# Exp of the scores from PSUM, Sign as conversion, scaled features signalled per chunk

## The chip, the cores and the metric

One of the NeuronCores of a Trainium2 chip runs the kernel. The metric is the time of an execution on the device in microseconds (us), as the median of several runs. Engines: PE multiplies matrices and writes PSUM; DVE (VectorE), ACT (ScalarE) and POOL (GpSimd) work elementwise; SP (SyncE) only issues transfers. ACT, SP and POOL each have a queue on which they issue DMA transfers. Engines wait for each other through semaphores. SBUF and PSUM have 128 partitions; PSUM has 8 banks of 512 fp32 per partition.

## What is computed

A graph attention layer with residual and layer norm: N = 4096 nodes, D = 128 features, a dense adjacency matrix of int32 (64 MB) with 0 and 1.

```
s_i = x @ attn[:128]; s_j = x @ attn[128:]
e = leaky_relu(s_i + s_j.T, negative_slope=0.2)
e = e + where(adj > 0, 0, -1e9)
y = x + softmax(e, axis=1) @ x
out = (y - mean(y)) / sqrt(var(y) + 1e-5)      # per row
```

## The kernel before

The softmax is taken apart. With m the largest s_j, exp(leaky(s_i + s_j)) is, up to a factor of the row i that falls out in the division, exp(0.2 (s_j - m)) times max(q_i, r_j), where r_j = exp(0.8 (s_j - m)) and q_i = exp(-0.8 relu(s_i + m)). So DVE makes, for a **chunk** c of 128 nodes j and a **block** n of 512 nodes i, the weights max(q_row, r_j) * mask in one scalar_tensor_tensor (`weigh`, L658), 128x512, and PE multiplies them by xj = d_j * x (with d_j itself as a 129th column for the denominator). Four matmuls (`product`, L784), one for each 128 of the 512 rows, sum into four PSUM banks; the trace shows each as two records. There are 8 blocks of 32 chunks, 256 chunks. `q_row` holds q for all i in 8 pieces of 512; block n uses piece n.

The adjacency comes in 32 **pieces** g of 2 MB, four to a block, each worth 8 chunks. A piece is four transfers of 512 KB: SP issues two (LOW_HALF), ACT two (HIGH_HALF), in `load_piece` (L251 in the trace), and piece g is issued only when piece g-2 has landed and its buffer is free. Pieces from 2 on are converted from int32 to uint8 by ACT (`to_bytes`, L388 and L393, as Sigmoid(200 x - 100)), pieces 0 and 1 by DVE (L567, L554). DVE turns the bytes (stream transpose, `turn` L549, `turn_half` L562) and then weighs. On DVE the order is written out: after the sixth chunk of piece g (TURN_AT = 5) comes the turn of piece g+1. For the pieces in HALVED conversion and turn go in two halves of four chunks, the second half being turned after chunk SECOND_HALF_AT. After chunk 13 of a block comes the residual of the block before (L591 to L609). Weights may run 12 chunks ahead of PE (W_SLOTS).

Before the loop: PE turns x (L758) and computes the scores s_i, the same on all partitions, in eight pieces of 512 into PSUM banks (`s_i_piece`, L769); DVE and ACT compute s_j, its maximum m (`smax`), below_max = s_j - m. ACT makes d_j, r_j, and then for each s_i piece Relu(score + m) into q_row (L365), and Exp(-0.8 q) in place, for piece 0 at once (`q_factors`, L371) and for the other seven in one instruction later. It scales x into xj in four stripes of 8 chunks (`scale_xj`, L377) and signals each stripe. PE begins the loop when stripe 0 is scaled, weights 0 are ready and four s_i pieces have left PSUM, since the loop's first four banks (0 to 3) hold scores until then.

ACT runs all this in program order, its transfers included: a `load_piece` is issued where it stands in ACT's program. After the loop over a block ACT and POOL normalise its rows and POOL stores them.

## Time and profile before

| | us |
|---|---|
| median of 3 runs | 267.55 |
| lowest, highest | 266.38, 269.02 |
| the profiled execution | 266.52 |
| its span, first to last instruction | 264.7 |

| engine | busy us | share |
|---|---|---|
| PE | 248.3 | 94% |
| DVE | 237.0 | 90% |
| ACT | 172.6 | 65% |
| POOL | 36.0 | 14% |

| costliest lines | what | count | busy us | mean ns |
|---|---|---|---|---|
| L784 PE | product | 2048 | 231.6 | 276 (overlapping) |
| L658 DVE | weigh | 256 | 171.4 | 741 |
| L393 ACT | conversion of a piece | 28 | 103.9 | 3709 |
| L549 DVE | turn of a piece | 29 | 36.0 | 1241 |

The transfers move 71.67 MB, 271 GB/s over the span. Times of single instructions are from the profiled execution and count from its span's start. Matmul records overlap, so their spacing and not their duration gives PE's rate; a few can be missing. "Idle before" is the time an engine stood before an instruction, with what ended it. PEclk is the granted clock of PE as a share of 2.4 GHz.

### The profile page before, as it was taken

How to read it: one execution, taken by the hardware profiler on the slowest of the kernel's cores; microseconds unless marked ns; L12 is line 12 of the kernel's file. 1: busy time of each engine (PE TensorE's matmuls, PEld its weight loads, DVE VectorE, ACT ScalarE, POOL GpSimd, SP SyncE). 2: the span in 40 equal slices, each digit the busy share in tenths (PEclk: the TensorE clock that was granted, in tenths of full speed). 3: DMA queues.
4: the chain of work that ended last, by engine and by line, in shares of the span. 5: the costliest groups of instructions: out<-in, count | busy, mean ns of one | idle time of the engine just before them, and what ended most of it. 6: DMA issues, size and time to landing. Idle time of an engine off the chain costs nothing.

```text
span 264.7 us, 5321 instructions
## 1 busy us (share of the span) xinstructions
PE 248.3 (94%) x2117; PEld 242.1 (91%) x2117; DVE 237.0 (90%) x382; ACT 172.6 (65%) x249; POOL 36.0 (14%) x75
## 2 busy tenths in 40 slices
PE   5894999999999999999999999999999999999980
PEld 5643999999999989999999999999999999999980
DVE  1889988699989899999999999999999999999652
ACT  1479998655496549755985579755975497566410
POOL 1000000000033001400042003300330023003413
PEclk9799899999999999999999999999999999999996
DMA  7999999999999999999999999999999999930101
GB/s 188 316 346 299 297 224 283 308 299 297 298 270 287 332 303 288 305 352 311 303 308 349 307 311 297 316 330 295 307 294 344 297 313 310 349 110 2 41 0 42
DMA packets 70172, 71.67 MB, mean 271 GB/s; under 512 B 2817, under 2 KB 68610, under 8 KB 70146
## 3 DMA queue, kind: packets, MB, share of 16 engines
q1 hardware_dynamic: 34562, 34.67, 47.5%
q10 hardware_dynamic: 34560, 34.67, 47.1%
q0 software_dynamic: 1024, 1.97, 2.4%
q8 instruction: 17, 0.28, 0.5%
q14 instruction: 9, 0.07, 0.1%
HBM read 69.21 MB, written 2.10 MB: 269 GB/s over the span
## 4 chain that ended last, share of the span: by engine, by line
PE 63%; DMA 23%; ACT 6%; ACTq 2%; DVE 2%; issue 1%; POOL 1%; SPq 0%; DVEq 0%
PE psum L784 60%; DMA adj_in<-in_adj_dram 21%; DMA x_raw<-in_x_dram 2%; PE psum L758 2%; ACT xj L377 2%; ACT q_row L365 2%; ACTq L251 2%; ACT mask_bytes L393 1%; PE psum L769 1%; POOL out_dram L259 1%; DVE mask_t L549 0%; ACT L388 0%; DVE x_raw L603 0%; ACT x_raw L451 0%; DVE weights L658 0%
## 5 line engine op out<-in xcount | busy, mean ns | idle before, releaser
L784 PEld LDWEIGHTS psum<-xj,weights 128*128 128x128 f32 x2048 | 230.8, 193 | 6.8 <-ACT xj L377 4.6
L784 PE MATMUL psum<-xj,weights 128*128 128x129 f32 x2048 | 231.6, 276 | 5.4 <-ACT xj L377 3.8
L658 DVE SCALAR_TENSOR_TENSOR weights<-q_row,r_j,mask_t 128x512 f32<-128x512 f32 x256 | 171.4, 741 | 0.1
L393 ACT ACTIVATE mask_bytes<-adj_in,sig_bias 128x4096 uint8<-128x4096 int32 x28 | 103.9, 3709 | 61.1 <-DMA adj_in<-in_adj_dram 60.9
L549 DVE STREAM_TRANSPOSE mask_t<-mask_bytes 128x1024 uint32<-128x1024 uint32 x29 | 36.0, 1241 | 6.9 <-ACT mask_bytes L393 6.5
L312 POOL TENSOR_SCALAR neg_mean<-total 128x4 f32<-128x4 f32 x7 | 1.6, 222 | 181.5 <-ACT x_raw L401 181.5
L321 POOL DMA_DIRECT2D out_dram<-x_raw x28 | 14.6, 526 | 21.5 <-ACT x_raw L415 21.4
L415 ACT ACTIVATE x_raw<-x_raw,offset,rstd 128x128 f32<-128x128 f32 x28 | 11.4, 479 | 2.8 <-POOL offset L318 2.8
L408 ACT ACTIVATE unused<-x_raw,neg_mean 128x128 f32<-128x128 f32 x28 | 10.9, 390 | 2.5 <-POOL neg_mean L312 2.5
L316 POOL TENSOR_TENSOR rstd<-variance,half 128x4 f32<-128x4 f32 x7 | 9.9, 1411 | 0.6
L377 ACT ACTIVATE xj<-x_raw,d_j 128x128 f32<-128x128 f32 x32 | 9.7, 390 | 0.0
L603 DVE SCALAR_TENSOR_TENSOR x_raw<-psum,rden,x_raw 128x128 f32<-128x128 f32 x32 | 9.2, 345 | 0.4
L758 PEld LDWEIGHTS psum<-ident,x_raw 128*128 128x128 f32 x32 | 5.1, 181 | 4.4 <-DMA x_raw<-in_x_dram 2.8
L388 ACT ACTIVATE mask_bytes<-adj_in,sig_bias 128x2048 uint8<-128x2048 int32 x4 | 7.8, 1995 | 1.0 <-DMA adj_in<-in_adj_dram 1.0
L401 ACT ACTIVATE x_raw<-x_raw 128x128 f32<-128x128 f32 x28 | 8.2, 293 | 0.0
L758 PE MATMUL psum<-ident,x_raw 128*128 128x128 f32 x32 | 6.0, 345 | 2.2 <-DMA x_raw<-in_x_dram 2.2
L769 PE MATMUL psum<-adj_in,attn_iw 128*128 128x512 f32 x16 | 7.7, 593 | 0.0
L348 ACT COPY adj_in<-psum 128x512 f32<-128x512 f32 x8 | 4.3, 579 | 3.7 <-PE psum L758 3.7
L512 DVE TENSOR_TENSOR adj_in<-x_raw,attn_j 128x1024 f32<-128x1024 f32 x4 | 4.7, 1218 | 2.0 <-DMA x_raw<-in_x_dram 2.0
L591 DVE TENSOR_SCALAR rden<-psum 128x4 f32<-128x4 f32 (+2 forms) x10 | 1.6, 156 | 5.2 <-PE psum L784 5.2
L459 ACT ACTIVATE deviations<-moments,eps 128x1 f32<-128x1 f32 x2 | 0.6, 294 | 8.5 <-DVE moments L627 8.5
L562 DVE STREAM_TRANSPOSE mask_t<-mask_bytes 128x512 uint32<-128x512 uint32 x6 | 4.3, 709 | 1.9 <-ACT mask_bytes L388 1.9
(61 smaller groups left out, 66.5 us busy)
## 6 DMA issues: line engine op xcount, KB each, us to landing
adj_in<-in_adj_dram ACTq DMA_DIRECT2D x64, 512.0 KB, 11.4
adj_in<-in_adj_dram SPq DMA_DIRECT2D x64, 512.0 KB, 10.0
out_dram<-x_raw POOLq DMA_DIRECT2D x28, 64.0 KB, 5.4
x_raw<-in_x_dram ACTq DMA_DIRECT2D x4, 256.0 KB, 5.9
x_raw<-in_x_dram SPq DMA_DIRECT2D x4, 256.0 KB, 6.8
out_dram<-x_raw POOLq DMA_DIRECT2D x4, 32.0 KB, 1.8
out_dram<-x_raw SPq DMA_DIRECT2D x4, 16.0 KB, 1.8
out_dram<-x_raw ACTq DMA_DIRECT2D x4, 16.0 KB, 2.1
```

The lines of the kernel that those rows point to most:

```text
L316: nc.gpsimd.tensor_tensor(rstd[:, 0:K], variance[:, 0:K], half[:, 0:K], ALU.pow).then_inc(rstd_ready, 1)
L321: pool.dma_start(out_v[g, q, :, :], x_raw[B * q:B * (q + 1), g * K:(g + 1) * K, :].rearrange("b k d -> b (k d)")).then_inc(stored, 16)
L377: last = nc.scalar.activation(xj[:, c, 0:D], x_raw[:, c, :], ACT.Copy, scale=d_j[:, c:c + 1])
L393: nc.scalar.activation(mask_bytes[:, g % BYTE_SLOTS, :, :, :], adj_in[:, g % ADJ_SLOTS, :, :, :], ACT.Sigmoid, bias=sig_bias[:], scale=200 ...
L408: last = nc.scalar.activation(unused[:, k, :], tile(g * K + k), ACT.Square, bias=neg_mean[:, k:k + 1], accum_out=square_sum[:, k:k + 1])
L415: last = nc.scalar.activation(tile(g * K + k), tile(g * K + k), ACT.Identity, bias=offset[:, k:k + 1], scale=rstd[:, k:k + 1])
L549: nc.vector.transpose(dst.rearrange("p f (r a) -> p r f a", a=B), src).then_inc(mask_ready, 1)
L603: nc.vector.scalar_tensor_tensor(tile(n * K + t), banks[(n * K + t) % 8][:, 0:D], rden[:, t:t + 1], tile(n * K + t), ALU.mult, ALU.add).th ...
L658: nc.vector.scalar_tensor_tensor(weights[:, slot_of(n, c), :], q_row[:, n * BANK:(n + 1) * BANK], r_j[:, c:c + 1], mask_t[:, (n * PIECES + ...
L758: last = nc.tensor.transpose(banks[XT_BANK + m % 4][:, k * P:(k + 1) * P], x_raw[:, m * K + k, :], ident[:])
L769: nc.tensor.matmul(banks[bank][:, :], attn_iw[:], xT[:, rb * BANK:(rb + 1) * BANK], start=True, stop=True).then_inc(s_i_in_psum, 1)
L784: return nc.tensor.matmul(banks[(n * K + t) % 8][:, 0:D1], weights[:, slot_of(n, c), t * P:(t + 1) * P], xj[:, c, 0:D1], start=(c == 0), s ...
```

## The change

- **q directly from PSUM.** smax gets a third column, -0.8 m, made by one more DVE operation. ACT computes Exp(-0.8 score - 0.8 m) from PSUM in one instruction per piece (`q_piece`); Relu and the Exp over SBUF are gone. Without the Relu q can be above 1, where it should be 1.
- **min in place of mult.** The weights are min(max(q, r), mask). The mask is 0 or 1 and r at most 1, so this is 0 where there is no edge and cuts q at 1 where there is one.
- **Sign in place of Sigmoid** in the conversion of the adjacency, without bias and scale; the memset of the bias goes.
- **xj per chunk.** ACT signals every scaled chunk, and PE waits in block 0 for the chunk that it needs. Chunk 0 is scaled right behind q piece 0, chunks 1 to 7 behind the fourth q piece, 8 to 11 before the first conversion; the other twenty follow in fours around the half conversions of pieces 2 and 3. The last four q pieces are made behind pieces 2 and 4.
- **The first matmuls in reverse order.** Chunk 0's four matmuls go to banks 3, 2, 1, 0, each waiting for one more q piece.
- **ACT's transfers.** The two quadrants of piece 2 are issued apart, behind q piece 0 and behind the second; piece 3 is issued behind chunk 7; for halved pieces, piece g+2 is issued between the halves.
- **Piece 4 is halved too,** and the second half is turned after the fourth chunk instead of the third. DVE waits for the q piece of its own block alone, PE for all eight at block 1.

```diff
@@ -45,8 +45,8 @@
     MASK_SLOTS = 6
     W_SLOTS = 12
     BY_DVE = 2
-    SECOND_HALF_AT = 2
-    HALVED = (0, 2, 3)
+    SECOND_HALF_AT = 3
+    HALVED = (0, 2, 3, 4)
     TURN_AT = 5
     RESIDUAL_AT = 13
     LAST = 8
@@ -104,7 +104,7 @@
         below_max = sb("below_max", [P, CHUNKS], fp32)
         r_j = sb("r_j", [P, CHUNKS], fp32)
         d_j = sb("d_j", [P, CHUNKS], fp32)
-        smax = sb("smax", [P, 2], fp32)
+        smax = sb("smax", [P, 3], fp32)
         rden = sb("rden", [P, T], fp32)
         total = sb("total", [P, T], fp32)
         neg_mean = sb("neg_mean", [P, T], fp32)
@@ -116,7 +116,6 @@
         moments = sb("moments", [P, T, 2], fp32)
         deviations = sb("deviations", [P, T], fp32)
         offset = sb("offset", [P, T], fp32)
-        sig_bias = sb("sig_bias", [P, 1], fp32)
         eps = sb("eps", [P, 1], fp32)
 
 
@@ -169,8 +168,8 @@
         max_spread = sem("max_spread")
         max_found = sem("max_found")
         below_max_ready = sem("below_max_ready")
+        max_scaled = sem("max_scaled")
         factors_ready = sem("factors_ready")
-        s_i_ready = sem("s_i_ready")
         q_ready = sem("q_ready")
         xj_scaled = sem("xj_scaled")
         bytes_ready = sem("bytes_ready")
@@ -301,7 +300,6 @@
             nc.gpsimd.affine_select(out=ident[:], in_=ident[:], compare_op=ALU.not_equal, fill=1.0, base=0,
                                     pattern=[[-1, P]], channel_multiplier=1).then_inc(consts_ready, 1)
             nc.gpsimd.memset(half[:], -0.5)
-            nc.gpsimd.memset(sig_bias[:], -100.0)
             nc.gpsimd.memset(eps[:], EPS)
             nc.gpsimd.memset(rden[:], 0.0)
             nc.gpsimd.memset(worst[:], 0.0).then_inc(worst_ready, 1)
@@ -359,41 +357,34 @@
             nc.scalar.activation(r_j[:], below_max[:], ACT.Exp, scale=1 - SLOPE)
             nc.scalar.activation(xj[:, :, D], below_max[:], ACT.Exp, scale=SLOPE)
 
-            def s_i_piece(rb):
+            def q_piece(rb):
 
                 act.wait_ge(s_i_in_psum, S_I_BY_PE.index(rb) + 1)
-                nc.scalar.activation(q_row[:, rb * BANK:(rb + 1) * BANK], banks[S_I_BANK[rb]][:, :],
-                                     ACT.Relu, bias=smax[:, 1:2]).then_inc(s_i_ready, 1)
-
-            def q_factors(first, stop):
-
-                act.wait_ge(s_i_ready, stop)
-                nc.scalar.activation(q_row[:, first * BANK:stop * BANK], q_row[:, first * BANK:stop * BANK], ACT.Exp,
-                                     scale=SLOPE - 1).then_inc(q_ready, stop - first)
-
-            def scale_xj(st):
-
-                for c in range(st * SC, (st + 1) * SC):
-                    last = nc.scalar.activation(xj[:, c, 0:D], x_raw[:, c, :], ACT.Copy, scale=d_j[:, c:c + 1])
-                last.then_inc(xj_scaled, 1)
-
-            def to_bytes(g):
+                nc.scalar.activation(q_row[:, rb * BANK:(rb + 1) * BANK], banks[S_I_BANK[rb]][:, :], ACT.Exp,
+                                     bias=smax[:, 2:3], scale=SLOPE - 1).then_inc(q_ready, 1)
+
+            def scale_xj(first, stop):
+
+                for c in range(first, stop):
+                    nc.scalar.activation(xj[:, c, 0:D], x_raw[:, c, :], ACT.Copy, scale=d_j[:, c:c + 1]).then_inc(xj_scaled, 1)
+
+            def bytes_may_go(g):
 
                 act.wait_ge(adj_loaded[g % ADJ_SLOTS], 16 * Q * (g // ADJ_SLOTS + 1))
                 if g >= BYTE_SLOTS:
                     act.wait_ge(mask_ready, g - BYTE_SLOTS + 1)
-                if g in HALVED:
-                    for f in range(PF):
-                        part = slice(f * P, (f + 1) * P)
-                        half_bytes = nc.scalar.activation(mask_bytes[:, g % BYTE_SLOTS, :, :, part],
-                                                          adj_in[:, g % ADJ_SLOTS, :, :, part],
-                                                          ACT.Sigmoid, bias=sig_bias[:], scale=200.0)
-                        half_bytes.then_inc(act_half_ready if f == 0 else bytes_ready, 1)
-                else:
-                    nc.scalar.activation(mask_bytes[:, g % BYTE_SLOTS, :, :, :], adj_in[:, g % ADJ_SLOTS, :, :, :],
-                                         ACT.Sigmoid, bias=sig_bias[:], scale=200.0).then_inc(bytes_ready, 1)
-                if g + IN_FLIGHT < ALL_PIECES:
-                    load_piece(act, HIGH_HALF, g + IN_FLIGHT)
+
+            def half_to_bytes(g, f):
+
+                part = slice(f * P, (f + 1) * P)
+                half_bytes = nc.scalar.activation(mask_bytes[:, g % BYTE_SLOTS, :, :, part],
+                                                  adj_in[:, g % ADJ_SLOTS, :, :, part], ACT.Sign)
+                half_bytes.then_inc(act_half_ready if f == 0 else bytes_ready, 1)
+
+            def to_bytes(g):
+
+                nc.scalar.activation(mask_bytes[:, g % BYTE_SLOTS, :, :, :], adj_in[:, g % ADJ_SLOTS, :, :, :],
+                                     ACT.Sign).then_inc(bytes_ready, 1)
 
             def sum_rows(g):
                 act.wait_ge(y_ready, g * K + K)
@@ -417,21 +408,40 @@
                 last.then_inc(out_ready, 1)
 
             act.wait_ge(worst_ready, 1)
-            s_i_piece(0)
-            q_factors(0, 1)
-            load_piece(act, HIGH_HALF, 2)
-            for rb in S_I_ORDER[1:4]:
-                s_i_piece(rb)
-            scale_xj(0)
-            for rb in S_I_ORDER[4:]:
-                s_i_piece(rb)
-            q_factors(1, RB)
+            act.wait_ge(max_scaled, 1)
+            q_piece(0)
+            load_piece(act, HIGH_HALF[0:1], 2)
+            act.wait_ge(factors_ready, 1)
+            scale_xj(0, 1)
+            q_piece(S_I_ORDER[1])
+            load_piece(act, HIGH_HALF[1:2], 2)
+            q_piece(S_I_ORDER[2])
+            q_piece(S_I_ORDER[3])
+            scale_xj(1, PC)
             load_piece(act, HIGH_HALF, 3)
-            scale_xj(1)
+            scale_xj(PC, PC + K)
             for g in range(BY_DVE, ALL_PIECES):
-                to_bytes(g)
-                if g < BY_DVE + 2:
-                    scale_xj(g)
+                bytes_may_go(g)
+                if g in HALVED:
+                    half_to_bytes(g, 0)
+                    load_piece(act, HIGH_HALF, g + IN_FLIGHT)
+                    if g < PIECES:
+                        scale_xj(g * PC - K, g * PC)
+                    half_to_bytes(g, 1)
+                    if g < PIECES:
+                        scale_xj(g * PC, g * PC + K)
+                else:
+                    to_bytes(g)
+                    if g + IN_FLIGHT < ALL_PIECES:
+                        load_piece(act, HIGH_HALF, g + IN_FLIGHT)
+                if g == PIECES - 2:
+                    q_piece(S_I_ORDER[4])
+                    q_piece(S_I_ORDER[5])
+                elif g == PIECES - 1:
+                    scale_xj(CHUNKS - K, CHUNKS)
+                elif g == PIECES:
+                    q_piece(S_I_ORDER[6])
+                    q_piece(S_I_ORDER[7])
                 if g % PIECES == PIECES - 1 and g > PIECES:
                     sum_rows(g // PIECES - 1)
                     sum_squares(g // PIECES - 1)
@@ -535,6 +545,7 @@
             nc.vector.reduce_max(smax[:, 1:2], banks[MAX_BANK][:, 0:P], X).then_inc(max_found, 1)
             dve.wait_ge(max_found, 1)
             nc.vector.tensor_scalar(below_max[:], s_j[:], smax[:, 1:2], None, ALU.subtract).then_inc(below_max_ready, 1)
+            nc.vector.tensor_scalar(smax[:, 2:3], smax[:, 1:2], SLOPE - 1, None, ALU.mult).then_inc(max_scaled, 1)
 
             def turn(g):
 
@@ -658,10 +669,10 @@
                 nc.vector.scalar_tensor_tensor(
                     weights[:, slot_of(n, c), :], q_row[:, n * BANK:(n + 1) * BANK], r_j[:, c:c + 1],
                     mask_t[:, (n * PIECES + c // PC) % MASK_SLOTS, c // K % PF, :, c % K],
-                    ALU.max, ALU.mult).then_inc(weights_ready, 1)
+                    ALU.max, ALU.min).then_inc(weights_ready, 1)
 
             for n in range(BLOCKS):
-                dve.wait_ge(q_ready, 1 if n == 0 else RB)
+                dve.wait_ge(q_ready, S_I_ORDER.index(n) + 1)
                 for c in range(CHUNKS):
                     g = n * PIECES + c // PC
                     if c % PC == 0 and g in HALVED:
@@ -788,17 +799,17 @@
             for n in range(BLOCKS):
                 last_chunks = LAST if n == BLOCKS - 1 else 0
                 for c in range(CHUNKS - last_chunks):
-                    if n == 0 and c % PC == 0:
-                        pe.wait_ge(xj_scaled, c // PC + 1)
+                    if n == 0:
+                        pe.wait_ge(xj_scaled, c + 1)
                     pe.wait_ge(weights_ready, n * CHUNKS + c + 1)
                     if c == 0:
-                        if n == 0:
-                            pe.wait_ge(s_i_ready, 4)
-                        elif n == 1:
-                            pe.wait_ge(s_i_ready, RB)
-                        else:
+                        if n == 1:
+                            pe.wait_ge(q_ready, RB)
+                        elif n > 1:
                             pe.wait_ge(y_ready, (n - 1) * K)
-                    for t in range(K):
+                    for t in reversed(range(K)) if n == 0 and c == 0 else range(K):
+                        if n == 0 and c == 0:
+                            pe.wait_ge(q_ready, K - t)
                         last = product(n, c, t)
                     last.then_inc(weights_used, 1)
             for t in range(K):
```

ACT from the first q piece on, before (x3 stands for three alike; the waits are in brackets):

```order
L365 ACTIVATE q_row<-psum,smax 128x512 [waits s_i_in_psum,worst_ready]
L371 ACTIVATE q_row<-q_row 128x512 [waits s_i_ready]
L251 DMA adj_in<-in_adj_dram 32x16x256 [waits adj_loaded0]
L251 DMA adj_in<-in_adj_dram 32x16x256
L365 ACTIVATE q_row<-psum,smax 128x512 [waits s_i_in_psum] x3
L377 ACTIVATE xj<-x_raw,d_j 128x128 x8
L365 ACTIVATE q_row<-psum,smax 128x512 [waits s_i_in_psum] x4
L371 ACTIVATE q_row<-q_row 128x3584 [waits s_i_ready]
L251 DMA adj_in<-in_adj_dram 32x16x256 [waits row_max_ready,adj_loaded1]
L251 DMA adj_in<-in_adj_dram 32x16x256
L377 ACTIVATE xj<-x_raw,d_j 128x128 x8
L388 ACT_TABLE_LOAD
```

and the same place of the changed program, up to the first conversion:

```order
L363 ACTIVATE q_row<-psum,smax 128x512 [waits s_i_in_psum,max_scaled,worst_ready]
L250 DMA adj_in<-in_adj_dram 32x16x256 [waits adj_loaded0]
L369 ACTIVATE xj<-x_raw,d_j 128x128 [waits factors_ready]
L363 ACTIVATE q_row<-psum,smax 128x512 [waits s_i_in_psum]
L250 DMA adj_in<-in_adj_dram 32x16x256 [waits adj_loaded0]
L363 ACTIVATE q_row<-psum,smax 128x512 [waits s_i_in_psum] x2
L369 ACTIVATE xj<-x_raw,d_j 128x128 x7
L250 DMA adj_in<-in_adj_dram 32x16x256 [waits row_max_ready,adj_loaded1]
L250 DMA adj_in<-in_adj_dram 32x16x256
L369 ACTIVATE xj<-x_raw,d_j 128x128 x4
L380 ACTIVATE mask_bytes<-adj_in 128x16x128 [waits adj_loaded2]
```

The four q pieces that free PE's banks are no longer followed by a stripe of eight scalings before PE may start; both transfers of piece 3 stand ahead of the four other q pieces, and the table load is gone.

ACT from the conversion of piece 3 to that of piece 4, before:

```order
L388 ACTIVATE mask_bytes<-adj_in,sig_bias 128x16x128 [waits mask_ready,adj_loaded3]
L388 ACTIVATE mask_bytes<-adj_in,sig_bias 128x16x128
L251 DMA adj_in<-in_adj_dram 32x16x256 [waits first_bytes_ready,adj_loaded3]
L251 DMA adj_in<-in_adj_dram 32x16x256
L377 ACTIVATE xj<-x_raw,d_j 128x128 x8
L393 ACTIVATE mask_bytes<-adj_in,sig_bias 128x4096 [waits mask_ready,adj_loaded4]
```

and now, with piece 4 in halves and q pieces behind it:

```order
L380 ACTIVATE mask_bytes<-adj_in 128x16x128 [waits mask_ready,adj_loaded3]
L250 DMA adj_in<-in_adj_dram 32x16x256 [waits first_bytes_ready,adj_loaded3]
L250 DMA adj_in<-in_adj_dram 32x16x256
L369 ACTIVATE xj<-x_raw,d_j 128x128 x4
L380 ACTIVATE mask_bytes<-adj_in 128x16x128
L369 ACTIVATE xj<-x_raw,d_j 128x128 x8
L380 ACTIVATE mask_bytes<-adj_in 128x16x128 [waits mask_ready,adj_loaded4]
L250 DMA adj_in<-in_adj_dram 32x16x256 [waits first_bytes_ready,adj_loaded4]
L250 DMA adj_in<-in_adj_dram 32x16x256
L380 ACTIVATE mask_bytes<-adj_in 128x16x128
L363 ACTIVATE q_row<-psum,smax 128x512 [waits s_i_in_psum] x2
```

Between the first half of piece 3 and that of piece 4 stand twelve scalings instead of eight, four of them between the halves.

## Rows read from the trace of the kernel before

**Rows 1.** Page: engines' busy time, and GB/s in 40 slices.

```profile
PE 248.3 (94%) x2117; PEld 242.1 (91%) x2117; DVE 237.0 (90%) x382; ACT 172.6 (65%) x249; POOL 36.0 (14%) x75
...
GB/s 188 316 346 299 297 224 283 308 299 297 298 270 287 332 303 288 305 352 311 303 308 349 307 311 297 316 330 295 307 294 344 297 313 310 349 110 2 41 0 42
```

**Rows 2.** Waits: who waited for whom: us in total, times, longest us.

```profile
ACT mask_bytes L393 <- DMA adj_in<-in_adj_dram: 60.9, 25, 4.3
...
PE psum L784 <- DVE weights L658: 1.6, 3, 0.7
```

**Rows 3.** Chain that ended last: start us, us, what.

```profile
33.72 14.01 DMA adj_in<-in_adj_dram
...
91.19 3.72 ACT mask_bytes L393
...
97.87 157.54 PE psum L784 x1408
```

**Rows 4.** Timeline, pieces 4 and 5: start us, us, engine line op, [idle before <-releaser].

```profile
47.76 3.71 ACT L393 ACTIVATE mask_bytes<-adj_in,sig_bias 128x4096 uint8<-128x4096 int32 x1 [1.01 <-DMA adj_in<-in_adj_dram]
...
51.50 1.25 DVE L549 STREAM_TRANSPOSE mask_t<-mask_bytes 128x1024 uint32<-128x1024 uint32 x1 [2.38 <-ACT mask_bytes L393]
...
53.43 14.56 PE L784 MATMUL psum<-xj,weights 128*128 128x129 f32 x128 [0.65 <-DVE weights L658]
...
54.73 3.71 ACT L393 ACTIVATE mask_bytes<-adj_in,sig_bias 128x4096 uint8<-128x4096 int32 x1 [3.27 <-DMA adj_in<-in_adj_dram]
```

**Rows 5.** Timeline, piece 9 to chunk 78.

```profile
84.18 3.71 ACT L393 ACTIVATE mask_bytes<-adj_in,sig_bias 128x4096 uint8<-128x4096 int32 x1 [2.00 <-DMA adj_in<-in_adj_dram]
...
87.99 1.25 DVE L549 STREAM_TRANSPOSE mask_t<-mask_bytes 128x1024 uint32<-128x1024 uint32 x1 [0.73 <-ACT mask_bytes L393]
...
94.43 0.15 DVE L591 TENSOR_SCALAR rden<-psum 128x4 f32<-128x4 f32 x1
...
95.95 1.24 DVE L549 STREAM_TRANSPOSE mask_t<-mask_bytes 128x1024 uint32<-128x1024 uint32 x1
```

**Rows 6.** Timeline of the start.

```profile
17.82 0.67 ACT L365 ACTIVATE q_row<-psum,smax 128x512 f32<-128x512 f32 x1
...
18.53 1.27 ACTq L251 DMA_DIRECT2D adj_in<-in_adj_dram  x2
...
19.41 2.08 DVE L658 SCALAR_TENSOR_TENSOR weights<-q_row,r_j,mask_t 128x512 f32<-128x512 f32 x3
19.85 1.84 ACT L365 ACTIVATE q_row<-psum,smax 128x512 f32<-128x512 f32 x3 [0.70 <-PE psum L769]
...
21.57 2.44 ACT L377 ACTIVATE xj<-x_raw,d_j 128x128 f32<-128x128 f32 x8
...
24.07 26.14 PE L784 MATMUL psum<-xj,weights 128*128 128x129 f32 x217 [3.82 <-ACT xj L377]
25.25 2.29 DVE L554 TENSOR_SCALAR mask_bytes<-adj_in 128x4096 uint8<-128x4096 int32 x1
...
26.82 1.29 ACTq L251 DMA_DIRECT2D adj_in<-in_adj_dram  x2
...
28.73 5.35 DVE L658 SCALAR_TENSOR_TENSOR weights<-q_row,r_j,mask_t 128x512 f32<-128x512 f32 x8
...
31.95 1.28 ACT L388 ACT_TABLE_LOAD   x1
...
33.24 2.00 ACT L388 ACTIVATE mask_bytes<-adj_in,sig_bias 128x2048 uint8<-128x2048 int32 x1
```

**Rows 7.** Windows: stretch, length, busy by engine (count), PEclk, DMA share, GB/s.

```profile
20.00:22.00 2.00, 0.25 (x1) 0.00 (x0) 2.00 (x4) 2.00 (x5) 0.00 (x0) 1.00 1.11 344
22.00:24.00 2.00, 0.00 (x0) 0.00 (x0) 1.97 (x4) 2.00 (x8) 0.00 (x0) 1.00 1.12 214
...
26.00:28.00 2.00, 2.00 (x12) 2.00 (x11) 1.97 (x2) 1.91 (x2) 0.00 (x0) 0.50 1.11 341
...
30.00:32.00 2.00, 2.00 (x20) 2.00 (x20) 2.00 (x4) 1.98 (x8) 0.00 (x0) 1.00 1.13 233
```


## Prediction

> **What bounds the kernel now.** [rows 1] first: PE is busy for 94% of the span, so I ask whether it is slow, late, or waiting. In the main loop it waits 3.8 us once for ScalarE's scaled xj, which is the loop's late start at 24.07 [rows 6], and 1.6 us in three waits for weights [rows 2]. ScalarE waits 60.9 us, 25 times, for the adjacency transfers. The chain that ended last says how these hang together [rows 3]: from 33.72 to 91.19 it consists of four transfers, each two pieces after the one whose landing lets it be issued (the first of them is shown), and only from 97.87 is it PE, without a hole, to the end: 1408 records in 157.54 us, 112 ns each. A chunk is four matmuls of two records, so 0.895 us, and a piece of 8 chunks 7.16 us. The transfers' own pace from 33.72 to 91.19 is 57.47 us for eight pieces, 7.18 us. So until 98 us two things run at the same pace: PE and the transfers.
>
> How a landing reaches PE is seen twice. Piece 4: conversion starts at 47.76, transposition at 51.50 after 2.38 us of idleness, PE goes on at 53.43 after 0.65 us [rows 4]; that is chunk 30, since DVE turns piece g+1 after the sixth chunk of piece g. Landing plus 5.7 us. Piece 9: conversion 84.18, turn 87.99, then eight chunks of weights, then the residual of the block from 94.43 on, the next turn at 95.95, PE at 97.87 [rows 5]: landing plus 13.7 us. From there PE's work is 178 chunks, fixed. **The end of the kernel is the landing of piece 9 plus 13.7 us plus PE's remaining work.** An earlier start helps only if that landing moves, or if it was PE that was late there.
>
> **The start, part by part** [rows 6]. One extra small DVE operation (smax times -0.8) stands ahead of DVE's first conversion: a DVE operation on 128x4 takes 0.15 [rows 5]; DVE's whole prologue shifts by 0.15, at most twice that. ScalarE: the first q piece is one Exp instead of Relu and Exp (the Relu takes 0.67), and four pieces are done after about 17.8 + 4 x 0.61 + one scaling of 0.30 + two issues in between that hold it up by some 0.1 to 0.6: at 20.8. (An Exp that reads PSUM isn't in the trace. Its neighbour is the Relu of the same tile, 1.84 for three: 0.61 from start to start, 0.67 alone. I take 0.61; the other bound adds 0.2 for four. The scaling is 2.44 for eight.) Weights 0 are ready at 19.41 + 0.15 + 0.75 = 20.3. So PE starts at 20.4 to 20.9 instead of 24.07, over 3 us earlier.
>
> What then is late? DVE. It makes the same things up to the conversion of piece 1 (25.25, 2.29 us), in another order (four, then two chunks instead of three and three), and chunk 6 is still weighed at 28.73 + 0.15, ready at 29.6. PE, now at full speed, has finished chunks 0 to 5 by about 26.6 and stands for 3 us. It used to reach chunk 6 at 24.07 + 6 x 0.895 + 1.8 = 31.2; the 1.8 are for the stretch at a granted clock of 0.50 (1.2 GHz, [rows 7]): 30 chunks took 53.43 - 24.07 = 29.36 us, less 26.85 at the full rate, less the wait of 0.65. So the 3.3 us at the start are 1.6 us at chunk 6. The new hole of 3 us may bring a stretch at 1.2 GHz of its own, as the hole of 3.82 did, for another 1.8.
>
> Next ScalarE. Its work from the first conversion on, in the new order: half of piece 2 (2.0, starts at 33.2 or when the piece lands; the table load of 1.28 at 31.95 lay in ScalarE's wait for that landing up to a tenth or two, so its removal is worth nothing there), four scalings (1.2), half, four scalings, two q pieces (1.2), then the first half of piece 3: 7.5 us after its start, at 40.5. Then half, 1.2, half, 2.4 for eight scalings: 7.5 us again, so the first half of piece 4 begins at 48.0 (before: 47.76, all of it). That is just the transfers' pace of 7.18 and 0.2 to 0.3 us over. PE needs scaled chunk 20 at 29.6 + 14 x 0.895 = 42.1 and gets it at 40.5 + 2.0 + 0.3 = 42.8, a small new wait. The Exp over seven pieces that is saved and the 1.28 of the table make room for all that; they are no gain of themselves, since ScalarE stood waiting 60.9 us.
>
> Piece 4 in halves: DVE's turn needs the first half alone, 48.0 + 2.0 = 50.0, then turn (0.6) and weights (0.75): chunk 30 is ready at 51.4 and PE, coming from chunk 20 at 42.8, takes it at 51.8 instead of 53.43. **At this point the change is 1.6 us ahead** (0.6 if the clock dropped). Block 1 waits for all eight q pieces: 50.0 + 2.0 + 1.3 = 53.3, and PE gets there at 51.8 + 1.8 = 53.6: hidden by 0.3 us.
>
> Now the cover ends. Piece 5 is converted whole: landing at 54.73 [rows 4], plus 5.7: PE gets chunk 38 at 60.4, and would be there at 51.8 + 7.2 = 59.0. Chunk 46 comes through DVE's chain at landing of piece 5 plus 13.7, chunk 78 likewise from piece 9. If the transfers stand where they stood, PE is at 97.87 again and nothing is gained; by the same token a mishap at the start of up to 1.4 us costs nothing.
>
> **What moves the transfers.** In 20 to 22 us the queues move 344 GB/s, in 22 to 24 214 and in 30 to 32 233 [rows 7]. ScalarE issues its half of piece 2 at 18.53 and of piece 3 at 26.82 [rows 6], and the low stretches lie about 4 to 5 us behind these issues. Now the first quadrant of piece 2 is issued with the first q piece, at 17.9 (0.6 earlier), and piece 3 behind chunk 7, at 23.0 (3.8 earlier). With the some 300 GB/s of most slices [rows 1] as the rate: 0.6 us x (344 - 214)/300 = 0.25 us, and 2 us x (344 - 233)/300 = 0.75 us. That is 1.0 us if the mean rate decides when a piece is complete, and 0.25 if its slowest share does, which can be late while the queue as a whole is nearly dry. I take 0.7. Below: nothing. Above: the slice of 33 to 40 us runs at 224 [rows 1]; if it too went to 344, it would add 6.6 x 120/300 = 2.6 us, 3.6 in all.
> The Trainium skill, "DMA: Bandwidth & Descriptors", section "Issuing engines are not separate DMA queues", says that transfers started by different engines run on the same 16 DMA engines, and that issuing from several saves only the issuing time. By it an earlier issue from ScalarE gives nothing and the sum would be 0; the trace disagrees in part, since the rate falls from 344 to 214 GB/s with one queue dry.
>
> Steady state: Sign for Sigmoid, without a bias operand. Not in the trace; the Sigmoid takes 3.71 for 4096 elements and 2.0 for 2048, that is 0.84 ns an element, which leaves 0.27 for everything else; a function without operand can at best save that, and I take no difference. Above, no row bounds it: rival C prices it. The min in place of mult in DVE's weighing: same operation class, 0. POOL loses a memset: 0. The tail is untouched.
>
> **Sum.** The profiled execution ran 266.52 us with a span of 264.7; it is 1.0 us below the median of 267.55. Minus 0.7: 265.8 against its own time, 266.8 against the median. I forecast 266.7.
>
> **Rivals.**
> A. The transfers come early enough and PE sets the pace. Chunk 30 at 51.8, chunk 78 at 51.8 + 48 x 0.895 = 94.8 instead of 97.87: 3.1 us, at most 3.9 (no wait at chunk 20), 2.1 with a clock drop: 264.4. It needs piece 5 at 53.2 and piece 9 at 81.1, 1.5 and 3.1 us early. For it: the slice at 224 GB/s. Against: between 33.72 and 91.19 the chain holds a steady 7.18 a piece whatever ScalarE does, and with issues tied to landings it catches up nothing. Chance 0.22.
> B. The transfers don't move at all, since the slowest share of piece 2 and not ScalarE's issue sets its landing: 267.5. Chance 0.17. The page's rule would have it so.
> C. Slower: Sign costs more than Sigmoid, or ScalarE's new order is dearer than I count. Between 33 and 48 us four half conversions, 16 scalings and two q pieces have no slack. Each 10% on a conversion delays the first half of piece 4 by 0.8 us, with it ScalarE's issue of piece 6 and the chain of landings behind it, and adds 0.37 at chunk 78: 1.2 us. At 6% it eats the gain; from about 28% it is over 1% slower; at 40%, 267.55 + 4.8 - 0.7 = 271.6. Against: the Sigmoid's time goes by elements, and so do the other activations'. Chance 0.11, with what else disturbs the transfers.
> The forecast (gain 0 to 2.6) has 0.50.
>
> **Numbers.** About 1% (2.7 us) is what a measurement of this kernel tells from no change; its three times spread over 2.6 us. Faster by over 1%: A and the forecast's edge, 0.24. Slower: C, 0.11. Within 1%: 0.65. Range: A's deeper end, 263.6, to B plus the spread of a median, 268.9; it leaves out C and the edges.
>
> **What would show it.** Right: PE's first main matmul near 20.5 to 21; a wait of about 3 us at 26.6; chunk 30 near 51.8; waits for weights at chunks 38, 46 and 78; the chain through transfers up to about 90 us, then 157.5 us of PE. The conversion of piece 9 starts at 83.5. Wrong: if PE runs through from 52 us without waits, A holds; if the conversion of piece 3 starts well after its landing, or one of 4096 elements is over 3.9 us, C; if piece 3 is on ScalarE before 38 us, my 0.7 is too small.

## The result and the profile after

| | median us | lowest to highest | runs |
|---|---|---|---|
| before | 267.31 | 266.15 to 270.06 | 20 |
| after | 265.31 | 262.64 to 267.00 | 20 |

The ratio is 0.9905, 95% interval 0.9878 to 0.9933: 2.0 to 2.5 us, 0.95%, faster. A ratio here and below leaves out executions more than 1.5% above the fastest of their kernel (three of the twenty here, eight of the twelve in one later run, and single ones of 522 and 374 us) and is not the quotient of the medians, which take in all. The profiled execution took 265.12 us with a span of 263.1 (before 266.52 and 264.7).

The page, engines' busy time and GB/s, beside [rows 1]:

```profile
PE 247.7 (94%) x2117; PEld 242.1 (92%) x2117; DVE 237.0 (90%) x384; ACT 164.9 (63%) x247; POOL 36.3 (14%) x74
...
GB/s 180 321 332 340 348 346 286 255 262 272 284 284 296 341 300 294 301 351 310 318 313 351 309 294 297 317 312 298 300 299 333 306 307 305 350 98 4 40 0 42
```

PE and DVE do the same work as before; ScalarE has 7.7 us less. The three slices from 20 to 39 us, 299, 297 and 224 GB/s before, are 340, 348 and 346 now. The waits, beside [rows 2] (us in total, times, longest):

```profile
ACT mask_bytes L386 <- DMA adj_in<-in_adj_dram: 63.0, 25, 4.4
...
ACT mask_bytes L380 <- DMA adj_in<-in_adj_dram: 3.5, 1, 3.5
...
PE psum L795 <- DVE weights L669: 2.8, 1, 2.8
```

PE's three waits for weights are one, of 2.8 us, at the start; those at chunks 30, 46 and 78 are gone. At chunk 78 it is close: DVE has those weights at 96.0, PE comes at 96.2. The chain (start, us, what), beside [rows 3]:

```profile
29.49 0.64 DVE weights L669
...
30.27 223.49 PE psum L795 x1984
```

There is no adjacency transfer in it any more: PE runs without a hole from chunk 6 to the end. The start and the first conversions, beside [rows 4] and [rows 6]:

```profile
18.06 0.59 ACTq L250 DMA_DIRECT2D adj_in<-in_adj_dram  x1
...
18.30 0.67 ACT L363 ACTIVATE q_row<-psum,smax 128x512 f32<-128x512 f32 x1
...
19.16 1.83 ACT L363 ACTIVATE q_row<-psum,smax 128x512 f32<-128x512 f32 x3
...
20.79 3.81 PE L795 MATMUL psum<-xj,weights 128*128 128x129 f32 x32
...
23.09 1.54 ACTq L250 DMA_DIRECT2D adj_in<-in_adj_dram  x2
...
25.49 2.02 PE L795 MATMUL psum<-xj,weights 128*128 128x129 f32 x16 [0.89 <-ACT xj L369]
25.92 2.29 DVE L565 TENSOR_SCALAR mask_bytes<-adj_in 128x4096 uint8<-128x4096 int32 x1
...
29.43 1.91 ACT L380 ACTIVATE mask_bytes<-adj_in 128x2048 uint8<-128x2048 int32 x1 [3.47 <-DMA adj_in<-in_adj_dram]
...
30.27 29.91 PE L795 MATMUL psum<-xj,weights 128*128 128x129 f32 x251 [2.75 <-DVE weights L669]
...
37.09 1.90 ACT L380 ACTIVATE mask_bytes<-adj_in 128x2048 uint8<-128x2048 int32 x1
...
44.22 1.91 ACT L380 ACTIVATE mask_bytes<-adj_in 128x2048 uint8<-128x2048 int32 x1
...
51.84 3.62 ACT L386 ACTIVATE mask_bytes<-adj_in 128x4096 uint8<-128x4096 int32 x1 [2.77 <-DMA adj_in<-in_adj_dram]
```

PE starts at 20.79 instead of 24.07 and then stands twice: 0.89 us before chunk 4 and 2.75 us before chunk 6, which DVE has ready at 30.1. Pieces 2, 3, 4 and 5 are on ScalarE at 29.43, 37.09, 44.22 and 51.84, where it was 33.24, 40.50, 47.76 and 54.73. Windows (stretch, length, busy by engine, PEclk, DMA share, GB/s), beside [rows 7]:

```profile
28.00:30.00 2.00, 0.00 (x0) 0.00 (x0) 1.97 (x3) 0.56 (x1) 0.00 (x0) 1.00 1.10 347
...
32.00:34.00 2.00, 2.00 (x11) 2.00 (x11) 2.00 (x4) 2.00 (x5) 0.00 (x0) 0.50 1.11 350
...
36.00:38.00 2.00, 2.00 (x20) 2.00 (x19) 2.00 (x5) 2.00 (x4) 0.00 (x0) 1.00 1.10 346
```

PE does nothing from 28 to 30, and two us later its granted clock is 0.50 (1.2 GHz) for a while: chunk 10 begins at 35.5, behind the 34.9 of before. And piece 9 on the way to chunk 78, beside [rows 5]:

```profile
82.39 3.62 ACT L386 ACTIVATE mask_bytes<-adj_in 128x4096 uint8<-128x4096 int32 x1 [2.41 <-DMA adj_in<-in_adj_dram]
...
86.11 1.25 DVE L560 STREAM_TRANSPOSE mask_t<-mask_bytes 128x1024 uint32<-128x1024 uint32 x1 [1.06 <-ACT mask_bytes L386]
...
94.06 1.24 DVE L560 STREAM_TRANSPOSE mask_t<-mask_bytes 128x1024 uint32<-128x1024 uint32 x1
```

### The profile page after: what moved, and what is told of

Same layout as the page of the kernel before. It is cut to its first block, busy times and chain, and to the rows that moved or that the text cites. A ratio compares the mean times of both kernels' runs of the same rounds, so it can differ in the third digit from the quotient of the medians.

```text
span 263.1 us, 5348 instructions
## 1 busy us (share of the span) xinstructions
PE 247.7 (94%) x2117; PEld 242.1 (92%) x2117; DVE 237.0 (90%) x384; ACT 164.9 (63%) x247; POOL 36.3 (14%) x74
## 4 chain that ended last, share of the span: by engine, by line
PE 88%; DVE 5%; DMA 2%; POOL 1%; issue 0%; ACT 0%; SPq 0%; DVEq 0%; ACTq 0%
PE psum L795 85%; DMA x_raw<-in_x_dram 2%; PE psum L769 2%; DVE weights L669 2%; PE psum L780 1%; DVE mask_bytes L578 1%; DVE mask_bytes L565 1%; POOL out_dram L258 1%; DVE mask_t L573 1%; DVE mask_t L560 0%; ACT x_raw L461 0%; DVE x_raw L614 0%; SPq L233 0%; SPq L271 0%; DVE half_moments L635 0%
## 5 line engine op out<-in xcount | busy, mean ns | idle before, releaser
L386 ACT ACTIVATE mask_bytes<-adj_in 128x4096 uint8<-128x4096 int32 x27 | 97.7, 3619 | 63.1 <-DMA adj_in<-in_adj_dram 63.0
L560 DVE STREAM_TRANSPOSE mask_t<-mask_bytes 128x1024 uint32<-128x1024 uint32 x28 | 34.8, 1242 | 6.6 <-ACT mask_bytes L386 6.5
L380 ACT ACTIVATE mask_bytes<-adj_in 128x2048 uint8<-128x2048 int32 x6 | 11.3, 1905 | 3.5 <-DMA adj_in<-in_adj_dram 3.5
L573 DVE STREAM_TRANSPOSE mask_t<-mask_bytes 128x512 uint32<-128x512 uint32 x8 | 5.6, 705 | 0.1
```

The costliest lines, as they stand in the source:

```text
L380: half_bytes = nc.scalar.activation(mask_bytes[:, g % BYTE_SLOTS, :, :, part], adj_in[:, g % ADJ_SLOTS, :, :, part], ACT.Sign)
L386: nc.scalar.activation(mask_bytes[:, g % BYTE_SLOTS, :, :, :], adj_in[:, g % ADJ_SLOTS, :, :, :], ACT.Sign).then_inc(bytes_ready, 1)
L560: nc.vector.transpose(dst.rearrange("p f (r a) -> p r f a", a=B), src).then_inc(mask_ready, 1)
```

## The experiments

Two things changed at once, the transfers and PE's start, and one new thing came, the hole with its slow clock. All ratios are to the kernel before, run beside; the runs up to the late start of PE shared one set of executions of it, the next four another, the next three a third, and the last a fourth. "Landing" below is when ScalarE begins to convert the piece, if it stood waiting for it; where it didn't, the issue that waits for the landing tells it.

**The changed kernel again**, as a yardstick.

> The changed kernel again, as the yardstick on this chip. Theory T (ScalarE's earlier issue of its half of piece 3 keeps both queues full up to 40 us, pieces 2 to 4 land 3.6 us earlier, and PE's three waits are gone) and theory S (the gain is PE's start, over 3 us earlier) say the same here: ratio 0.990 to before, span about 263, PE with no wait after chunk 6 at 30.3.

Measured: 265.47 us, ratio 0.9933 (0.9909 to 0.9956). Its profiled execution (267.24 us) is another one than the first, though:

```profile
84.69 3.62 ACT L386 ACTIVATE mask_bytes<-adj_in 128x4096 uint8<-128x4096 int32 x1 [2.31 <-DMA adj_in<-in_adj_dram]
...
98.29 3.95 PE L795 MATMUL psum<-xj,weights 128*128 128x129 f32 x33 [0.53 <-DVE weights L669]
```

Its prologue ended 1 us later (chunk 0 at 21.8), piece 2 landed at 32.0 and piece 9 at 84.69, and PE waits before chunk 78 as it did before the change, 13.60 us after that landing. So the changed kernel is bound by PE in one of its two profiled executions and by the transfers in the other. The late prologue goes with PE's clock: here it is granted 0.50 from 8 to 14 us, in the first profile 0.50 to 0.70 from 8 to 12, and DVE waits 2.78 us instead of 0.87 for what PE makes of the partial maxima.

**Late issue of piece 3.** In the changed kernel:

```diff
             scale_xj(1, PC)
-            load_piece(act, HIGH_HALF, 3)
             scale_xj(PC, PC + K)
+            act.wait_ge(weights_ready, 6)
+            load_piece(act, HIGH_HALF, 3)
```

> The changed kernel, ScalarE's half of piece 3 issued only when six weights are made, near 26.1 instead of 23.1 us (before: 26.8); all else as changed. T: the rate drops to about 215 to 235 GB/s near 30 us again, piece 2 lands near 33 instead of 29.4, PE waits near chunks 30, 46 and 78 again, and most of the gain goes: 1.3 to 2 us above the changed kernel, ratio to before 0.996 to 1.0. S: no difference to the changed kernel, ratio 0.990. Rival R (not piece 3 but the two quadrants of piece 2, issued 0.5 us earlier, moved the landings): piece 2 still lands near 29.4, ratio 0.990.

Measured: 265.92 us, ratio 0.9939 (0.9911 to 0.9967): 0.45 us above the yardstick, with intervals that overlap, where T had 1.3 to 2. In the profile the issue is at 26.4.

```profile
30.00:32.00 2.00, 1.33 (x12) 1.36 (x13) 2.00 (x4) 1.89 (x2) 0.00 (x0) 1.00 1.13 208
...
34.00:36.00 2.00, 2.00 (x21) 2.00 (x20) 2.00 (x4) 2.00 (x5) 0.00 (x0) 1.00 1.14 216
```

The low rates are back, and piece 3 lands at 39.9 instead of 36.9 to 37.1; but piece 2 lands at 30.1, which T had at 33. PE waits at chunks 38, 46 and 78. On the rates, piece 3 and PE's waits T is right. On piece 2, which landed early in spite of the late issue, and on the time R is: taking the early issue of piece 3 back costs nothing that these runs resolve.

**Early issue of piece 3 in the kernel before**, the one edit:

```diff
             scale_xj(0)
+            load_piece(act, HIGH_HALF, 3)
             for rb in S_I_ORDER[4:]:
                 s_i_piece(rb)
             q_factors(1, RB)
-            load_piece(act, HIGH_HALF, 3)
```

> The kernel before with one edit: ScalarE issues its half of piece 3 right behind the first stripe of scalings, near 23.9 instead of 26.8 us. T: pieces 2 to 4 land some 2 to 3 us earlier, the three waits of PE (2.3 us with their restarts) go, PE still starts at 24.1: ratio 0.991 to 0.993. S: 1.0. R: piece 2 lands at 33 as before, ratio 1.0.

Measured: 266.2 us, ratio 0.9955 (0.9929 to 0.9982): 0.45% from moving one line, which is half of the change's gain by its first measurement (0.95%) and two thirds by its second (0.67%). The issue comes at 22.79, as soon as piece 1 has landed. The timeline near chunk 78, and two windows:

```profile
83.04 3.71 ACT L393 ACTIVATE mask_bytes<-adj_in,sig_bias 128x4096 uint8<-128x4096 int32 x1 [2.08 <-DMA adj_in<-in_adj_dram]
...
96.72 5.51 PE L784 MATMUL psum<-xj,weights 128*128 128x129 f32 x47 [0.53 <-DVE weights L658]
```

```profile
22.00:24.00 2.00, 0.00 (x0) 0.00 (x0) 1.97 (x4) 2.00 (x8) 0.00 (x0) 1.00 1.13 213
30.00:32.00 2.00, 2.00 (x20) 2.00 (x19) 2.00 (x4) 2.00 (x8) 0.00 (x0) 1.00 1.10 349
34.00:40.00 6.00, 6.00 (x56) 6.00 (x55) 4.39 (x8) 6.00 (x11) 0.00 (x0) 1.00 1.12 229
```

The rate of 30 to 32 us is 349 instead of 233; the other two low stretches stay. Piece 2 lands at 32.2, piece 3 at 38.7, piece 9 at 83.0. T's direction holds, S (1.0) falls, and so does R as the only cause; but R isn't wrong either. In the seven profiled executions in which ScalarE first issues for piece 2 at 17.91 to 18.45 us, piece 2 lands at 29.4 to 30.7; in the seven with that issue at 18.52 to 19.30 (the kernel before, this one, the changed kernel's second, and four below) at 31.4 to 33.1.

**Late start of PE**, in the changed kernel:

```diff
-                        pe.wait_ge(xj_scaled, c + 1)
+                        pe.wait_ge(xj_scaled, max(c + 1, PC))
```

> The changed kernel, but PE waits for eight scaled chunks before chunk 0, so it begins near 23.1 instead of 20.8. T: it reaches chunk 6 at 30.3 all the same, since DVE makes those weights at 30.1: no difference to the changed kernel beyond where the granted clock falls (within 0.5 us). S: 2.3 us slower than the changed kernel, ratio 0.998.

Measured: 264.08 us, ratio 0.9914 (0.9877 to 0.9951): not slower. Five of the nine executions took 263.5 to 264.1 us and four 265.9 to 267.3; the profiled one is the fastest. Timeline and a window:

```profile
22.99 5.63 PE L795 MATMUL psum<-xj,weights 128*128 128x129 f32 x48 [2.36 <-ACT xj L369]
...
30.19 4.03 PE L795 MATMUL psum<-xj,weights 128*128 128x129 f32 x34 [1.57 <-DVE weights L669]
```

```profile
32.00:34.00 2.00, 2.00 (x20) 2.00 (x20) 2.00 (x5) 2.00 (x3) 0.00 (x0) 1.00 1.10 346
```

2.2 us of start thrown away, and chunk 6 is at 30.19 as before. The hole is 1.57 us instead of 2.75, and in this execution the clock stays at 1.00. S, which had 0.998, falls: the early start, the most visible part of the change, is worth nothing that these runs show.

**PE kept busy.** The fifth q piece is made before the first conversion, and behind chunk 5 PE turns the identity 11 times into its bank:

```diff
+                    if n == 0 and c == TURN_AT:
+                        pe.wait_ge(q_ready, K + 1)
+                        for _ in range(FILL):
+                            nc.tensor.transpose(banks[XT_BANK][:, 0:P], ident[:], ident[:])
```

> The changed kernel with 11 transpositions of the identity on PE behind chunk 5, into the bank of the fifth q piece, which is made early for it; they fill PE's hole of 2.8 us before chunk 6. Nothing is left out. Theory C (the new hole brings a stretch at granted clock 0.5 behind it in part of the executions, which costs 1.8 us; PE is the bound afterwards): no such stretch after 20 us, PE at chunk 10 near 33.8 instead of 35.5, 1 to 1.5 us faster than the changed kernel, ratio to before 0.987, and a narrower spread. Theory D (the transfers decide whatever the clock does): PE waits 1 to 2 us longer at chunk 78 instead, ratio 0.992 as the changed kernel.

Measured: 263.25 us, ratio 0.9865 (0.9819 to 0.9911), 2.2 us below the yardstick by the medians, 1.8 by the ratios, whose intervals just touch (with that of the first measurement they overlap); no clock of 0.50 after 20 us in the profile. The profiled execution is one of those with a late prologue:

```profile
28.52 1.36 PE L819 MATMUL psum<-ident 128*128 128x128 f32 x11
...
31.44 2.81 PE L796 MATMUL psum<-xj,weights 128*128 128x129 f32 x23 [1.56 <-DVE weights L670]
```

```profile
82.72 3.62 ACT L387 ACTIVATE mask_bytes<-adj_in 128x4096 uint8<-128x4096 int32 x1 [2.11 <-DMA adj_in<-in_adj_dram]
...
96.32 5.85 PE L796 MATMUL psum<-xj,weights 128*128 128x129 f32 x50 [0.21 <-DVE weights L670]
```

Chunk 78 again waits, 13.60 us behind the landing of piece 9. The median agrees with C, this execution with D. That the transpositions kept the clock up is not shown, since two of the four profiled executions with the unfilled hole of 2.75 us had no drop either (late issue of piece 3, and piece 4 whole). The spread (262.8 to 266.5) isn't narrower.

**Piece 4 whole**, HALVED = (0, 2, 3) in the changed kernel.

> The changed kernel with piece 4 converted and turned whole, as before. C and D: PE had more than 3 us of weights in hand there, so no difference within 0.5 us, ratio 0.992. Theory H (halving piece 4 carries a good part of the gain): 1 us or more slower than the changed kernel, ratio 0.996.

Measured: 264.9 us, ratio 0.9911 (0.9878 to 0.9943). H falls; halving piece 4 does nothing here.

**Half of piece 1 by ScalarE**, in its idle time before piece 2 (left out below: the semaphore, and that the issue of piece 6 waits for it too):

```diff
             load_piece(act, HIGH_HALF, 3)
+            act.wait_ge(adj_loaded[1], 16 * Q)
+            nc.scalar.activation(mask_bytes[:, 1, :, :, 0:P], adj_in[:, 1, :, :, 0:P], ACT.Sign).then_inc(act_first_ready, 1)
...
-                nc.vector.tensor_scalar(mask_bytes[:, g, :, :, :], adj_in[:, g, :, :, :], 0.0, None,
+                nc.vector.tensor_scalar(mask_bytes[:, g, :, :, P:], adj_in[:, g, :, :, P:], 0.0, None,
                                         ALU.is_gt).then_inc(first_bytes_ready, 1)
+                dve.wait_ge(act_first_ready, 1)
```

> The changed kernel, ScalarE converts the first half of piece 1 in its idle 3.5 us before piece 2, VectorE the second. Chunk 6 ready near 29.0 instead of 30.1, PE's hole 1.7 instead of 2.8 us. C: the clock falls in fewer executions, and PE is 1.1 us earlier: 1 to 2 us faster than the changed kernel, ratio 0.986 to 0.989. D: 0.992, unchanged.

Measured: 263.52 us, ratio 0.9849 (0.9815 to 0.9884). The start and chunk 78:

```profile
29.16 3.03 PE L801 MATMUL psum<-xj,weights 128*128 128x129 f32 x25 [1.76 <-DVE weights L675]
```

```profile
82.61 3.62 ACT L389 ACTIVATE mask_bytes<-adj_in 128x4096 uint8<-128x4096 int32 x1 [2.41 <-DMA adj_in<-in_adj_dram]
...
96.20 5.96 PE L801 MATMUL psum<-xj,weights 128*128 128x129 f32 x51 [0.53 <-DVE weights L675]
```

Chunk 6 is 1.1 us earlier; then PE waits at chunks 46, 62, 70 and 78, for the landings.

**Both of them.**

> Both of the preceding: half of piece 1 by ScalarE, and 6 transpositions in what is left of the hole. C: chunk 10 near 32.7, 1.1 us ahead of the run with transpositions alone, then PE meets the landings again and waits near chunk 78: ratio 0.984 to 0.987. D: 0.992.

Measured: 264.71 us, ratio 0.9892 (0.9848 to 0.9936), executions from 263.0 to 268.3. The two don't add up. Its profile is of the slowest execution and can't stand for the median; it has chunk 6 at 30.5 and then PE waits at five places; piece 9 lands at 85.57 and chunk 78 is at 99.17: 13.60 again.

**Late start and half of piece 1.**

> The changed kernel with ScalarE converting the first half of piece 1 and PE waiting for eight scaled chunks before chunk 0. PE begins near 23.0, chunk 6 is ready at 29.1, so the hole is some 0.8 us. Theory E (chunk 78 starts at the landing of piece 9 plus 13.7 us, or when PE gets there, whichever is later; what is gained at the start beyond the landing is lost again): no granted clock of 0.5 behind the hole, yet chunk 78 at the landing of piece 9 plus 13.7; ratio to before 0.984 to 0.988, no better than the runs with one of the two. Theory C alone (the clock and the hole are all that is left): PE at chunk 78 near 93.5 without waits, ratio 0.982.

Measured: 265.16 us, ratio 0.994 (0.9905 to 0.9974); the profiled execution was among the fastest, 263.35 us, with piece 9 at 80.42, chunk 78 at 94.01 (13.59) and no slow clock after 20 us. The median is worse than that of the half alone, which neither theory has. The profile of a fast execution can't show why; it stays open.

**Three pieces in flight, kernel before:** IN_FLIGHT = 3, and ScalarE issues its half of piece 4 right behind that of piece 3.

> The kernel before with three pieces in flight instead of two: each piece is issued when the one three before it has landed, ScalarE's half of piece 4 right behind that of piece 3. Nothing else is changed. E: the queues stay full through the loop, the rate is near 345 GB/s until the five buffers are full, piece 9 lands before 80 us, PE has no wait after 24.1 and its end is 24.07 + 256 x 0.8934 + 1.8 for the clock = 254.6 (before: 256.9): ratio 0.991. If the rate in the loop is bound by something else than the issue (15% below the peak whatever is queued): landings move by under 1 us, ratio 0.997 to 1.0.

Measured: 268.34 us, ratio 1.0058 (1.0035 to 1.0081): slower. A window of the loop, the start, and piece 9:

```profile
60.00:80.00 20.00, 20.00 (x182) 20.00 (x181) 19.93 (x34) 15.35 (x24) 3.45 (x6) 1.00 1.10 348
```

```profile
26.82 5.63 ACTq L251 DMA_DIRECT2D adj_in<-in_adj_dram  x4
...
32.49 0.69 ACT L377 ACTIVATE xj<-x_raw,d_j 128x128 f32<-128x128 f32 x2 [2.90 <-issue]
...
34.99 13.18 PE L785 MATMUL psum<-xj,weights 128*128 128x129 f32 x112 [1.88 <-ACT xj L377]
...
78.59 3.69 ACT L393 ACTIVATE mask_bytes<-adj_in,sig_bias 128x4096 uint8<-128x4096 int32 x1
```

The landings do what E says: 348 GB/s from 60 to 80 us instead of 291, piece 9 on ScalarE at 78.59 instead of 84.18 (it landed at 76.5, when SP issues piece 12), and no wait of PE from chunk 17 on. But ScalarE's issues take 5.63 us for four, and after that mostly 4.7 to 5.7 us for each pair, against mostly 1.3 to 1.5 before: it stands 2.90 us in "issue", scaled chunk 8 is late, and PE loses 1.88 us there. With the clock drop and a second small wait at chunk 16, chunk 78 comes at 97.9, where the landings had put it before.

**Three in flight on top of late start and half:**

> The run with late start and half of piece 1 by ScalarE, with three pieces in flight on top. E: the landings are out of the way, PE has no wait after chunk 6 at 29.2, chunk 78 near 93.6, end of PE near 252.5: span 260.2, ratio 0.978 to 0.981. If three in flight move nothing: as the run without it, 0.984 to 0.988.

Measured: 268.98 us, ratio 0.9995 (0.9952 to 1.0038). Here the median says more: it is 1.7 us above the 267.27 of the kernel before beside it, and 3.8 above the run without the third piece. The held issues again, and longer:

```profile
23.33 6.93 ACTq L253 DMA_DIRECT2D adj_in<-in_adj_dram  x2
...
30.30 1.91 ACT L427 ACTIVATE mask_bytes<-adj_in 128x2048 uint8<-128x2048 int32 x1 [6.59 <-issue]
...
34.27 3.94 PE L802 MATMUL psum<-xj,weights 128*128 128x129 f32 x20 [3.29 <-DVE weights L676]
```

Two issues hold ScalarE for 6.93 us, its half of piece 1 comes at 30.30 (24.5 to 24.9 with two in flight), PE stands 3.29 us and meets two stretches of slow clock.

**Three in flight from piece 7 on**, with both edits at the start:

```diff
-                landed = g - IN_FLIGHT
+                landed = g - IN_FLIGHT - (g >= THIRD_FROM)
...
                     q_piece(S_I_ORDER[7])
+                    load_piece(act, HIGH_HALF, THIRD_FROM)
...
-                    if g + IN_FLIGHT < ALL_PIECES:
-                        load_piece(act, HIGH_HALF, g + IN_FLIGHT)
+                    if g + IN_FLIGHT + 1 < ALL_PIECES:
+                        load_piece(act, HIGH_HALF, g + IN_FLIGHT + 1)
```

> The run with both edits (half of piece 1 by ScalarE, transpositions in PE's hole) and, from piece 7 on, three pieces in flight instead of two; the first seven pieces are issued as in the changed kernel, so that neither piece 1 nor ScalarE's first conversions are held up as in the run with three in flight from the start. E (chunk 78 starts at the landing of piece 9 plus 13.7 us or when PE gets there): the rate is near 345 GB/s from about 55 us on, piece 9 lands 3 us or more before PE needs it, and there is no wait at chunk 78; those at chunks 38 and 46 can stay, by piece 5. Chunk 78 near 94 to 95, ratio to before 0.980 to 0.984, and a narrower spread than with two in flight. If more in flight costs ScalarE more than it gives: 0.989, as without it, or worse.

Measured: 263.31 us, ratio 0.9851 (0.9818 to 0.9883), executions from 262.2 to 264.5. A window, piece 9 and the chain:

```profile
55.00:80.00 25.00, 25.00 (x227) 25.00 (x226) 24.14 (x39) 17.14 (x25) 4.08 (x7) 1.00 1.10 348
```

```profile
78.02 3.60 ACT L391 ACTIVATE mask_bytes<-adj_in 128x4096 uint8<-128x4096 int32 x1
```

```profile
28.65 0.64 DVE weights L678
...
29.43 221.85 PE psum L804 x1984
```

Piece 9 lands at 76.3 (SP's issue of piece 12) and is on ScalarE at 78.02, the chain has no adjacency transfer, chunk 78 is at 93.7. It is faster than the kernel before by 1.5%, and by some 0.5% than the changed kernel with its 0.9905, though these two intervals overlap a little; the ratio is just above the 0.980 to 0.984 that I gave. Against the run with half of piece 1 alone (0.9849) the median is the same, so that the third piece in flight adds anything to the time is not shown.

The profiled executions by the rule "chunk 78 = landing of piece 9 + 13.6, or PE when it gets there" (times in us):

| kernel | piece 9 on ScalarE | chunk 78 | difference | wait there |
|---|---|---|---|---|
| before | 84.18 | 97.87 | 13.69 | yes |
| after | 82.39 | 96.2 | 13.8 | no |
| after again | 84.69 | 98.29 | 13.60 | yes |
| late issue of piece 3 | 83.66 | 97.26 | 13.60 | yes |
| before, early issue | 83.04 | 96.72 | 13.68 | yes |
| late start | 80.02 | 94.5 | 14.5 | no |
| PE kept busy | 82.72 | 96.32 | 13.60 | yes |
| piece 4 whole | 81.95 | 95.55 | 13.60 | yes |
| half by ScalarE | 82.61 | 96.20 | 13.59 | yes |
| both | 85.57 | 99.17 | 13.60 | yes |
| late and half | 80.42 | 94.01 | 13.59 | yes |
| third from piece 7 | 78.02 | 93.7 | 15.7 | no |

Where three are in flight from the start, piece 9 is on ScalarE at 78.59 and 75.76, chunk 78 is at 97.9 and 100.0, and PE doesn't wait there either. Where PE doesn't wait, chunk 78 is reckoned back from the end of PE's chain. The 0.09 between Sigmoid and Sign kernels is that of the conversion.

## Why the prediction was right, and where it was not

The time, 265.31, lies in the range of 263.6 to 268.9, 1.4 us under the forecast of 266.7, and the change is within 1% of before (0.95%), as forecast. That is owed in part to a wide range: the gain is 2.0 to 2.5 us where the sum had 0.7 to 0.9, and two of the signs that it was to be wrong by came true in the first profile, PE without a wait from 52 us on and piece 3 on ScalarE before 38 us. By its steps:

- **"The end is the landing of piece 9 plus 13.7 us plus PE's remaining work": right,** as one of two times of which the later one holds; the other is when PE gets there. Nine of the twelve executions above obey it to 0.01 us once the conversion's 0.09 is taken off; in the other three PE was later.
- **The start: right, and right that it is worth nothing.** PE at 20.79 (said 20.4 to 20.9), four q pieces at about 20.9, chunk 6 ready at 30.1 (29.6, with a prologue that ended 0.46 us later in this execution), a hole of 2.75 (3), and a stretch at 1.2 GHz that cost 1.6: the 72 chunks from 6 to 78 took 65.95 us, in the last run, without such a stretch, 64.31. The late start of PE costs nothing that is seen. The small wait for scaled chunk 20 (said 0.7) did not come.
- **Chunk 30: said 51.8, or 0.6 ahead of 53.43 with a clock drop; measured 53.4,** reckoned back from PE's chain, and not ahead at all. The prologue's 0.46 us make most of the difference.
- **What the transfers move: the step that failed.** I had taken 0.7 us, with bounds of 0 and 3.6. In the first profile pieces 2 to 4 were on ScalarE 3.8, 3.4 and 3.5 us earlier, which is the upper bound, and piece 9 1.8; in the second pieces 2 to 4 by 1.2, 0.8 and 0.5, and piece 9 was 0.5 later, behind a prologue that ended 1.5 us later than before. The sum priced each low stretch of the rate by its own length. It left the stretch of 33 to 40 us to the upper bound, but that is no thing of its own: both queues issue piece 4 only when all of piece 2 has landed, and by then have little left. Where piece 2 landed at 29.4 (after, late start) the rate stays at 343 to 351 GB/s up to 38 us; where it landed at 31.4 and 32.2 (PE kept busy, before with early issue) it is 231 to 252 and 229 there, with piece 3 issued early in both. So of the two issues that moved, the one of piece 3 gives 0.45% in the kernel before, but in the changed kernel taking it back costs only 0.06%, within the noise; the two don't add up, and how the gain divides between them stays open. The landing of piece 2 is the other part, of which the runs don't show whether the 0.5 us of its issue or something else in the prologue moves it. Half of the lead at piece 4 is lost again by piece 9: from piece 5 to 9 the first profile takes 30.55 us, the kernel before 29.45, and from 40 to 80 us its rate is 269 to 275 GB/s instead of 291 to 296. Why it falls behind there is open; it has two pieces in flight, and with three the rate is 348.
- **Rival A, at 0.22, was the better description of the first profile:** PE sets the pace, and 2.1 us of gain with a clock drop; chunk 78 came 1.7 us earlier in it, and the medians differ by 2.0. The forecast's mechanism, the wait at chunk 78, holds in the second profile. I had treated as exclusive what differs from one execution to another.
- **Rival B (nothing moves) is out; with it goes what the Trainium skill's page "DMA: Bandwidth & Descriptors" ("Issuing engines are not separate DMA queues") would give here.** It says that issuing from several engines saves only issuing time. Moving one issue of ScalarE forward by 4.0 us, in the kernel before and with nothing else, gave 0.45%, and the rate in the stretch went from 233 to 349 GB/s. That the transfers of both queues share the same engines is not contradicted by any run.
- **Rival C (dearer Sign): out.** 3.62 us against 3.71 for a piece, 1.91 against 2.0 for a half. In the first profile ScalarE was never late for piece 3 or 4: it began pieces 3 and 4 within 0.2 us of their landings, its other work ending just then. That it has no slack there was right.
- **The Exps over `q_row` (3.8 us), the table load (1.3) and the shorter conversions (2.7)** make up the 7.7 us that ScalarE has less. They are not on the path, as said; what they gave is the place for the two issues. The eight instructions that read the scores from PSUM take as long as the Relus did (5.0 and 4.9 us).
